# Integer tanh through a casting DMA, the mean subtracted on ScalarE, and token work spread over FFN tiles

## The reference

```python
x = x + xattn(layernorm(x), ctx, Wq, Wkv, Wout)   # softmax over 64 keys, causal mask
x = x + ffn(layernorm(x), w1, g1, w2, g2, w3, g3)
# ffn: h = silu(lin(x, w1, g1)) * lin(x, w2, g2); return lin(h, w3, g3), hidden width 1024
def linear_bit(x, w, g):
    return einsum('bsd,od->bso', act_quant(rmsnorm(x, g)), ternary_quant(w))
def act_quant(x):     scale = 127 / clip(max|x|, 1e-4); round(x * scale) / scale
def ternary_quant(w): s = mean|w|; round(tanh(w / (s + 1e-8))) * arctanh(s)
```

## Time and profile before

| | us |
|---|---|
| three runs, median (lowest, highest) | 202.84 (201.66, 203.04) |
| the profiled execution, its own time | 202.36 |
| its span, first to last instruction | 200.6 |
| busy: PE, DVE, ACT, POOL | 148.5, 164.4, 142.9, 130.0 |

### The profile page before, as it was taken

One profiled execution on the slowest core, in us unless ns is written; L12 is line 12 of the kernel. 1 busy time (PEld: TensorE's weight loads), 2 busy tenths in 40 slices (PEclk: granted clock), 3 DMA queues, 4 the chain that ended last, 5 costly groups with the idle time before them and its releaser, 6 DMA issues.

```text
span 200.6 us, 3287 instructions
## 1 busy us (share of the span) xinstructions
PE 148.5 (74%) x1082; PEld 97.3 (49%) x1082; DVE 164.4 (82%) x309; ACT 142.9 (71%) x195; POOL 130.0 (65%) x212
## 2 busy tenths in 40 slices
PE   5979886888779499697789764284888778775380
PEld 5567655676566377475557341131353243332360
DVE  1179799999788947999959598985989999999950
ACT  2026978985699586895769976696799998896220
POOL 4063727279885883877625669879878988997100
PEclk9999999999969958999699998557699999999588
DMA  5999920000000000000000000220234635534311
GB/s 167 320 379 423 400 117 0 7 0 0 3 2 0 3 0 0 3 0 0 0 3 2 0 0 0 52 52 5 52 80 88 149 82 115 120 78 100 83 54 54
DMA packets 20944, 15.02 MB, mean 75 GB/s; under 512 B 15296, under 2 KB 19648, under 8 KB 20416
## 3 DMA queue, kind: packets, MB, share of 16 engines
q1 hardware_dynamic: 20704, 14.42, 24.9%
q10 hardware_dynamic: 224, 0.39, 0.6%
HBM read 9.04 MB, written 2.10 MB: 56 GB/s over the span
## 4 chain that ended last, share of the span: by engine, by line
DVE 41%; POOL 15%; ACT 14%; PE 14%; issue 12%; DMA 2%; DVEq 0%; POOLq 0%; ACTq 0%
DVE c_max L1160 7%; DVE hh L1136 7%; ACT q_x L812 5%; ACT probs L769 4%; POOL u L434 4%; DVE u_max L1041 4%; PE bank L580 3%; POOL half_sum L404 3%; DVE hT L1147 3%; DVE row_max L962 3%; DVE y L1187 3%; DVE row_sum L975 2%; ACT probsT L754 2%; PE wide L587 2%; DMA out<-y 2%
## 5 line engine op out<-in xcount | busy, mean ns | idle before, releaser
L685 PE MATMUL wide<-wT,xqT 128*128 128x512 bf16 x128 | 36.0, 428 | 7.9 <-DVE hh L1136 6.7
L456 POOL TENSOR_TENSOR c_h<-hh,g3b 128x1024 f32<-128x1024 f32 x15 | 35.4, 2361 | 3.4 <-DVE hh L1136 3.3
L404 POOL TENSOR_TENSOR half_sum<-probs 128x512 f32<-128x512 f32 x16 | 20.3, 1270 | 24.9 <-ACT probs L769 24.9
L685 PEld LDWEIGHTS wide<-wT,xqT 128*128 128x128 bf16 x128 | 12.7, 107 | 25.8 <-issue 9.5
L705 PE MATMUL bank<-wT,hT 128*128 128x256 bf16 x112 | 15.9, 289 | 10.4 <-DVE hT L1147 10.4
L580 PE MATMUL bank<-woutT,attnT 128*128 128x256 f32 x64 | 20.0, 466 | 4.2 <-DVE attnT L983 4.2
L885 ACT ACTIVATE sq_junk<-hh,root_x 128x1024 bf16<-128x1024 f32 x16 | 18.3, 1147 | 5.3 <-DVE hh L1136 4.6
L769 ACT ACTIVATE probs<-probs,ln_rstd 128x1024 f32<-128x1024 f32 x16 | 18.4, 1152 | 4.9 <-DVE probs L968 4.8
L812 ACT ACTIVATE q_x<-u,round_c,qs_x 128x256 f32<-128x256 f32 x32 | 16.6, 588 | 7.1 <-issue 3.6
L434 POOL TENSOR_TENSOR u<-xc,g 128x512 f32<-128x512 f32 x16 | 20.0, 1272 | 2.4 <-ACT q_x L812 2.4
L968 DVE TENSOR_TENSOR probs<-wide,row_max 128x1024 f32<-128x1024 f32 x16 | 19.3, 1217 | 1.7 <-PE bank L506 1.6
(11 more groups left out here) (122 smaller groups left out, 303.3 us busy)
## 6 DMA issues: line engine op xcount, KB each, us to landing
out<-y SPq DMA_DIRECT2D x16, 128.0 KB, 2.0
x_sb<-in_x SPq DMA_DIRECT2D x1, 1280.0 KB, 10.3
xT<-in_xT SPq DMA_DIRECT2D x1, 1280.0 KB, 17.5
w_in<-in_w1T SPq DMA_DIRECT2D x1, 1024.0 KB, 12.3
w_in<-in_w2T SPq DMA_DIRECT2D x1, 1024.0 KB, 11.4
w_in<-in_w3T SPq DMA_DIRECT2D x1, 1024.0 KB, 13.5
x_sb<-in_x SPq DMA_DIRECT2D x1, 512.0 KB, 6.4
xT<-in_xT SPq DMA_DIRECT2D x1, 512.0 KB, 7.2
```

The source lines that it names most:

```text
L404: last = g.tensor_tensor(out=half_sum[:, t, :, :], in0=e[:, :, 0, :], in1=e[:, :, 1, :], op=ALU.add)
L456: g.tensor_tensor(out=c_h[:, t, :], in0=hh[:, t, :], in1=g3b[:], op=ALU.mult).then_inc(c_ready, 1)
L685: last = nc.tensor.matmul(wide[:, (w * 2 + n) * 512:(w * 2 + n + 1) * 512], xqT_cols(T, w * DC + c), w_cols[:, c, n * 512:(n + 1) * 512], ...
```

## The change

It has four parts. **Weights:** ACT writes each tanh as int16 into `tern`, which is the memory of `q_h` and holds one weight; the conversion rounds. POOL issues a DMA that copies `tern` to `wT` and converts int16 to bfloat16; it replaces DVE's `ternary`. Before the tanh of weight i > 0, ACT waits for the DMA of weight i-1. The three tanh move into iterations 3, 4 and 5 of ACT, behind `recip_T_copy`; POOL issues the DMAs in its iterations 4, 5 and 6, behind `keys`. **Mean:** `centre` moves from DVE to ACT for all batches and writes mean - x; the sign is turned back where the transposed integers are copied to `xqT`. **Order in attention:** PE projects before it transposes tokens; DVE takes the maxima of batch 1 before the sums of batch 0; the logarithm and the series of arctanh move. **Token work:** batches 5, 6 and 7 each get three FFN slots, from T = 1 on (`tokens_of(T)`), one step in each slot; the first slots are written in another order, and DVE's division and residual of batch 7 lie between the first products.

```diff
+        tanh_ready = sem("tanh_ready")
...
+        FIRST = 5
...
+        def tokens_of(T):
+
+            return FIRST + (T - 1) // 3, (T - 1) % 3
...
+        tern = q_h[:].rearrange("p t n -> p (t n)")
...
+                def ternary(i):
+
+                    need(pool, tanh_ready, i + 1)
+                    g.dma_start(wT[:, i * WN:(i + 1) * WN], tern).then_inc(tern_ready[i], 16)
...
+                def scaled_tile(b, t):
+                    need(pool, xc_ready, b + 1)
+                    need(pool, qx_ready, 2 * b - 1 + t)
+                    g.tensor_tensor(out=u[:, t, :, :], in0=xc[:, t, :].unsqueeze(1).to_broadcast([P, 2, D]),
+                                    in1=g12[:], op=ALU.mult).then_inc(u_ready, 1)
...
                     if live(j + 2):
                         keys(j + 2)
+                    if 0 <= j - 4 < 3:
+                        ternary(j - 4)
                     if from_(j, 2):
                         scaled(j - 2)
+                    if j == 2:
+                        series((11, 9, 7, 5))
+                    if j == 3:
+                        series((3, 1))
+                    if j == 4:
+                        log_branch()
                     if live(j + 1):
                         half_sums(j + 1)
...
                 def slot(T, t, b):
+                    a, step_ = tokens_of(T)
                     if live_tile(T) and not last_tile(T):
                         gained(T, t)
-                    if t == 0 and late(b + AHEAD):
-                        factor(b + AHEAD)
-                        scaled(b + AHEAD)
                     if live_tile(T):
                         scales(T, t, b)
-                    if t == 1 and late(b + AHEAD):
-                        token_scale(b + AHEAD)
+                    if T > 0 and a < B:
+                        if step_ == 0 and a > FIRST:
+                            factor(a)
+                        if step_ < 2:
+                            scaled_tile(a, step_)
+                        else:
+                            token_scale(a)
...
@@ -640,11 +661,11 @@
                     probs_T(j, 0)
                     if j == 0:
                         values_of(6, bank5)
+                    if from_(j, 1):
+                        project(j - 1)
                     if from_(j, 3):
                         need(pe, rT_ready, j)
                         tokens_T(j - 3, bank5)
-                    if from_(j, 1):
-                        project(j - 1)
                     probs_T(j, 1)
...
-                pe.wait_ge(tern_ready, 3)
+                for i in range(3):
+                    pe.wait_ge(tern_ready[i], 16)
...
-                    if t == 0 and late(b + AHEAD - 1) and b > 0:
-                        tokens_T(b + AHEAD - 1, hT_banks[b % 2])
-
-
+                    a, step_ = tokens_of(T)
+                    if step_ == 0 and a - 1 < B:
+                        tokens_T(a - 1, hT_banks[a % 2])
+
+
+                probs_T(7, 0)
                 need(pe, shifted, 2 * B)
                 up(0, 0, 0, 0)
-                up(0, 0, 0, 1)
-                probs_T(7, 0)
                 project(6)
                 probs_T(7, 1)
-                up(1, 1, 0, 0)
+                up(0, 0, 0, 1)
                 weigh(7)
                 recip_T(7)
-                tokens_T(4, bank7)
-                slot(0, 0, 0)
+                up(1, 1, 0, 0)
+                up(1, 1, 0, 1)
                 project(7)
-                tokens_T(5, bank7)
-                need(pe, bank4_free, B)
+                up(2, 0, 1, 0)
                 schedule(slot)
...
                 def weight_tanh(i):
 
 
-                    a.activation(w_in[:, bass.ds(i * WN, WN)], w_in[:, bass.ds(i * WN, WN)], ACT.Tanh,
+                    if i > 0:
+                        act.wait_ge(tern_ready[i - 1], 16)
+                    a.activation(tern, w_in[:, bass.ds(i * WN, WN)], ACT.Tanh,
                                  scale=w_inv[:, bass.ds(i, 1)]).then_inc(tanh_ready, 1)
...
-                                 ACT.Identity, bias=round_c[:, 1:2]).then_inc(xqT_ready, 1)
+                                 ACT.Identity, scale=-1.0, bias=round_c[:, 2:3]).then_inc(xqT_ready, 1)
+
+                def centre(b):
+
+                    need(act, b_stats, b + 1)
+                    need(act, u_ready, 2 * b)
+                    for t in range(TB):
+                        last = a.activation(xc[:, t, :], x_sb[:, tile_cols(b, t)], ACT.Identity, scale=-1.0,
+                                            bias=fb_mv[:, t, 0:1])
+                    last.then_inc(xc_ready, 1)
...
                 def iteration(j):
                     if from_(j, 2):
                         recip_T_copy(j - 1)
+                    if 0 <= j - 3 < 3:
+                        weight_tanh(j - 3)
                     if from_(j, 3):
                         quantise(j - 3)
...
                     if live(j + 2):
                         query_copy(j + 2)
+                    if from_(j, 1):
+                        centre(j - 1)
...
-                act.wait_ge(inv_ready, 1)
-                weight_tanh(0)
+                act.wait_ge(ln_in, 1)
+                a.activation(w_ln[:], w_ln[:], ACT.Ln).then_inc(ln_out, 1)
...
-                act.wait_ge(ln_in, 1)
-                a.activation(w_ln[:], w_ln[:], ACT.Ln).then_inc(ln_out, 1)
-                iteration(3)
-                weight_tanh(1)
-                iteration(4)
-                weight_tanh(2)
-                iteration(5)
+                centre(1)
+                act.wait_ge(inv_ready, 1)
+                for j in range(3, B - 2):
+                    iteration(j)
...
-                    if t == 0 and late(b + AHEAD - 1) and b > 0:
-                        quantise(b + AHEAD - 1)
-                    if t == 1 and late(b + AHEAD - 1) and b > 0:
-                        tokens_T_copy(b + AHEAD - 1, hT_banks[b % 2])
+                    a, step_ = tokens_of(T)
+                    if step_ == 0 and a - 1 < B:
+                        tokens_T_copy(a - 1, hT_banks[a % 2])
+                    if step_ == 0 and FIRST < a < B:
+                        centre(a)
+                    if step_ == 2 and a < B:
+                        quantise(a)
...
+                probs_T_copy(7, 0)
                 silu(0, 0, 0)
-                probs_T_copy(7, 0)
                 probs_T_copy(7, 1)
+                recip_widen(7)
+                square(0, 0, 0)
+                recip_T_copy(7)
+                silu(1, 1, 0)
                 quantise(4)
-                recip_widen(7)
-                silu(1, 1, 0)
-                recip_T_copy(7)
-                tokens_T_copy(4, bank7)
-                square(0, 0, 0)
-                quantise(5)
-                tokens_T_copy(5, bank7)
+                centre(5)
                 schedule(slot)
...
-                def ternary(i):
-                    need(dve, tanh_ready, i + 1)
-                    v.tensor_scalar(wT[:, i * WN:(i + 1) * WN], w_in[:, i * WN:(i + 1) * WN],
-                                    ROUND, ROUND, ALU.add, ALU.subtract).then_inc(tern_ready, 1)
...
                 def aggregate_sum(b):
 
+                    need(dve, xc_ready, b)
                     for t in range(TB):
                         last = v.bn_aggr(fb_mv[:, t, :], fb_bn[:, t, :])
                     last.then_inc(b_stats, 1)
 
-                def centre(b):
-
-                    need(dve, b_stats, b + 1)
-                    for t in range(TB):
-                        last = v.tensor_scalar(xc[:, t, :], x_sb[:, tile_cols(b, t)], fb_mv[:, t, 0:1], None,
-                                               ALU.subtract)
-                    last.then_inc(xc_ready, 1)
...
                         weight_scales()
-                    if isinstance(j, int) and j == B - 2:
-                        divide(j)
                     if from_(j, 1):
                         measure_sum(j - 1)
                     if front:
                         token_max(j - 2)
+                    if j == B - 2:
+                        divide(j)
                     elif from_(j, 1):
                         need(dve, b_bn, 2)
                     if from_(j, 1):
                         aggregate_sum(j - 1)
-                        centre(j - 1)
                     if front:
                         token_recip(j - 2)
...
-                sums(0)
                 maximum(1, 0)
                 maximum(1, 1)
+                sums(0)
                 shift(1, 0)
                 shift(1, 1)
                 for b in range(5, B):
                     measure(b)
                     aggregate(b)
-                iteration(1)
-                iteration(2)
-                iteration(3)
-                ternary(0)
-                iteration(4)
-                ternary(1)
-                iteration(5)
-                ternary(2)
+                for j in range(1, B - 2):
+                    iteration(j)
```

(34 more changed lines are left out.)

49 lines of the change are left out of this document (20 added, 29 removed).

## The result

The changed kernel took 206.50 us (median of 4 runs, 205.69 to 207.42), the kernel before 202.55 beside it (4 runs, 201.66 to 203.04): ratio 1.020, 95% interval 1.014 to 1.026. It is slower, where no change was forecast (202.4); the time lies inside the range, for other reasons than the range was drawn for. Its profiled execution took 205.69 us with a span of 203.8; before it was 202.36 and 200.6.

What follows compares the result with a forecast made beforehand. DVE was busiest (82%) and led the chain of waits; after the change, POOL's or ACT's list was to limit most stages. Terms -1.3 -1.7 -1.3 +2.1 +4.4 -8.1 +4.0 +2.0 = +0.1 on 202.36 gave 202.4 us, range 196.5 to 207.5.

Steps and rivals of the forecast that it cites:

- Start and iteration 3: Attention: start to batch 2's row sums -1.3 us, limited by POOL's half sums; iteration 3 -1.3, limited by ACT's list.
- The wait in iterations 4 and 5: Attention: ACT's tanh waits for POOL's previous rounding DMA, 17.5 us per iteration: +2.1 and +4.4 us.
- L: Attention: time from issue to landing of POOL's converting rounding DMA, taken as 3.5 us.
- To the second product: From batch 6's row sums to the second gated product: ACT's list, then less work between products, together -8.1 us.
- The tiles: FFN, second to last gated product: POOL's token work for three batches sets the time, +4.0 us.
- Links: Whole kernel: semaphore steps between engines and slow TensorE after new idle time, +2.0 us (0 to 4).
- A: Rival, whole kernel: the waits eat the gain, no change, 202.4 us; chance 0.36.
- B: Rival, attention and tiles: short transfer (2.0 us) and no links term, faster, 197.4 us; chance 0.32.
- C: Rival, iterations 4 and 5: POOL reaches its DMA early enough, so no wait, 190.4 us; chance 0.05.
- D: Rival, iterations 4 and 5: slow transfer of 6.4 us holds ACT's tanh, 208.2 us; chance 0.18.
- E: Rival, iterations 4 and 5: DVE holds POOL while it prepares the DMA, 207.0 us; chance 0.03.
- F: Rival, FFN tiles: slow TensorE clock lengthens nine spread tiles by 0.7 us each, 208.7 us; chance 0.06.

Runs made afterwards that it cites:

- e1: Changed kernel with two int16 memories for the tanh in turn, so only the third tanh waits for a DMA: 193.93 us, ratio 0.969 to the kernel before.
- e2: Changed kernel, one int16 memory, with POOL issuing each rounding DMA one iteration sooner: 194.91 us, ratio 0.977 to the kernel before.
- e3: Changed kernel with ACT's token quantisation in the tiles one slot later, its transposes and copy too: 200.69 us, ratio 1.003 to the kernel before.
- e9: Changed kernel with TensorE's attention order as before, token transposes ahead of the projection: 211.25 us, ratio 1.054 to the kernel before.
- e5: Changed kernel with the edits of e2 and e3 together: 188.32 us, ratio 0.941 to the kernel before.
- e7: e5 with TensorE's attention order as before, token transposes ahead of the projection: 191.43 us, ratio 0.957 to the kernel before.
- e4: Changed kernel with the weights part undone, float tanh in place and DVE rounding after iterations 3 to 5: 197.72 us, ratio 0.987 to the kernel before.
- e8: e5 with POOL leaving out, in the tiles, the half of u multiplied by g2: 186.71 us, ratio 0.933 to the kernel before.

## Why the prediction was wrong, point by point

**Start and iteration 3: right. Iteration 2: 1.0 too low.** -1.10, -0.72 and -1.47 for -1.3, -1.7 and -1.3. In iteration 2 DVE waits 1.93 us for POOL's half sums, as predicted, and POOL's operations came out 0.3 longer than my sum. The other 0.6 is what the sum left out: POOL stood 0.64 us idle before the second half sum, until ACT's second exponential was there.

**The wait in iterations 4 and 5: right in mechanism and place, and in size but for 1.0 us in iteration 5.** The chain "DMA behind POOL's half sums and keys, tanh behind the DMA, everything of ACT behind the tanh" is shown by the trace and by e1 and e2, which remove it in two ways. Iteration 4 took 17.37 for 17.5. L was 3.15 and 3.05 us; the 3.5 taken from rows was 0.4 high. The Trainium skill (DMA: Bandwidth & Descriptors, section on the anatomy of one DMA on the SWDGE path) gives 2.0 us plus bytes over 436e3 per us, an estimate of 3.2 us; the trace agrees.

**Iteration 5: 0.9 too low.** It took 18.38. The row sums of batch 6 stand behind the dequantisation factors of four batches, which my sum leaves out; DVE's timeline:

```profile
97.57 0.14 DVE L1070 RECIPROCAL rm_x<-u_max 128x4 f32<-128x4 f32 x1
97.71 0.45 DVE L1078 TENSOR_TENSOR m_x<-u_max,fb_a 128x16 f32<-128x16 f32 x1
...
98.90 0.40 DVE L1090 TENSOR_SCALAR bound_x<-bound_x,w_down 128x8 f32<-128x8 f32 x1
```

From 97.71 to 99.22 are 1.5 us. Without the waits iteration 5 is still 1.06 longer than iteration 4 (e2).

**To the second product: right.** 19.01 for 18.3, so -7.4 for -8.1. ACT's list counted from rows was good to 0.7.

**The tiles: this step failed.** The prediction put "POOL pays for each token scale 0.6, factor 1.5 and u 2.5 ... thus **+4.0**"; it was +8.2, and these 4.2 us are more than the 3.2 by which the span grew. I priced the tiles by the load of one engine. As a load the term holds: with the quantisation moved (e3) the tiles took 65.14 for a forecast 66.1. It even counts 1.5 too much, since `factor(5)` runs ahead of the tiles (`a > FIRST`) and only two factors stand in them; without it the forecast is 64.6. What the term left out is order: ACT's quantisation stands in the same slot as the POOL instruction that it needs, ahead of the next tile's silu. In attention I had followed exactly such a chain step by step; in the tiles I added up. The change's order of instructions showed it: `quantise(a)` in ACT's slot `step_ == 2`, `token_scale(a)` in POOL's, behind `scales`. With this one loss removed (e3) the ratio is 1.003, the "no change" that was forecast.

**Links, +2.0: not there as a term of their own.** Their place is taken by the 1.0 in iteration 2, 0.9 in 5 and 0.7 ahead of the second product; that these come near 2.0 in sum is luck. The rest of the profiled span, which was to stay, is 1.6 shorter; the output DMA above gives 2.0 of that and 0.4 go the other way. Summed: -1.1 -0.7 -1.5 +2.0 +5.3 -7.4 +8.2 -1.6 = +3.2.

**TensorE's order, given no term: wrong reason.** I wrote that ACT's list is longer anyway. The list is the limit only because the new order is there: undoing it costs 4.7 us of span in the change (e9) and 3.4 in e5 (e7). The iterations came out right since I had, without saying it, costed them with the projection out of the way.

**The rivals.** A came in attention and not in the tiles. B's short transfer was not there: L was 3.1, about a quarter of the way from 3.5 to 2.0. C was not seen, but e2 shows that it was one place in POOL's list away. D needed L above 4.7 and is refuted. E is refuted: POOL spent 0.79 and 0.64 on a DMA and DVE's work beside it kept its length (two maxima in 2.34 us both times, which read PSUM, as the rival itself said). F is refuted as a cause: the granted clock was 0.66 of 2.4 GHz at 130 to 140 us, 0.60 before, and e3 takes 5.1 us out of the tiles by order alone, at 0.87 over the tiles for the change's 0.90. Its mechanism, DVE behind a slower TensorE, shows in e1 and e4, whose tiles are 1.9 and 1.6 us longer. The time fell on the side "slower", which had 0.27, and inside the range, by a mechanism that no rival had: luck, not foresight.

## What to carry to other kernels

Give every stage the same treatment: for each instruction that a change puts into an in-order queue, ask what releases it, when that is issued on its own engine, and what ready work stands behind it. A sum of one engine's load is a lower bound for the stage, and two engines that wait for each other in one slot miss it: here ACT stood idle 2.8 to 3.6 us each time, of which 0.9 to 2.4 reached the time of the tiles. Two rules of order paid in this kernel. A result of another engine was better consumed one slot later than it is made (e3, 5.1 us), and a DMA whose source is reused was better issued ahead of an instruction that waits for the engine that reuses it (e2, 12 us).

## What the runs showed of the hardware

- A DMA from POOL that converts 512 KB of int16 to bf16 landed 3.0 us after its issue (median of three) and held POOL's own queue for 0.79 us the first time and 0.64 to 0.66 after it (the change, e2, e5).
- A tanh of 128x2048 that writes int16 took 2.00 us on ScalarE in the change, for 2.02 when it wrote float32 in place before.
- The granted clock of the same stretch differed between kernels: from 66 to 106 us it was 0.83 in the change, with TensorE busy 26.4 of 40 us, and 1.00, the full 2.4 GHz, in e5, with 34.1 of 40. The busy time of a stretch alone does not tell it: from 118 to 128 us it was 0.53 in e1 with TensorE busy 7.4 of 10 us, and 1.00 in e5 with 5.5.
- The same rounding of 128x2048 on VectorE took 1.20, 1.91 and 2.00 us (e4), each beside work of POOL, and in the first case POOL's half sum took 2.32 us instead of 1.27. m_x, a 128x16 product, took 0.16 us in the kernel before, 0.45 in the change and 1.23 in e5.
- On POOL a multiplication of 128x512 took 1.27 us and one of 128x256 0.72 (e5 and e8).
